# The last expert feed-forward placed among the events of the last attention, gated on its second-layer activations, and row maxima prepared two units ahead

## The reference, cut to what matters

```python
rh = relu(features @ router_w1 + router_b1)
expert_logits = softmax(rh @ router_w2 + router_b2)
top_w, top_i = top_k(expert_logits, 2)
routing_weights = softmax(top_w)
h1 = relu(einsum('bsd,edh->bseh', features, expert_w1) + expert_b1)
h2 = relu(einsum('bseh,ehf->bsef', h1, expert_w2) + expert_b2)
expert_out = einsum('bsef,efo->bseo', h2, expert_w3) + expert_b3
...
combined = sum(sel * routing_weights[..., None], axis=2)
```

## Time and profile before

| what | value |
|---|---|
| three runs | 1465.64, 1471.26, 1472.61 us, median 1471.26 us |
| profiled execution | 1465.17 us, of which the trace spans 1463.1 us |
| busy over the span | PE 80%, DVE 60%, ACT 42%, POOL 42% |
| mean granted clock of TensorE | 0.864 of full speed |
| first attention | from 79 to 860 us |
| second attention | from 940 to 1319 us |
| last feed-forward | from 1319 us to the end |

### The profile page before, as it was taken

How to read it: one execution, slowest core, us unless ns; L and a number is a source line. 1 busy time by engine, 2 the same in 40 slices (tenths; PEclk the granted TensorE clock), 3 DMA queues, 4 the chain that set the end, 5 groups by cost and what they waited for, 6 DMA issues and landing times.

```text
span 1463.1 us, 26112 instructions
## 1 busy us (share of the span) xinstructions
PE 1167.1 (80%) x9805; PEld 769.0 (53%) x9805; DVE 875.2 (60%) x1807; ACT 614.5 (42%) x1249; POOL 608.9 (42%) x1193
## 2 busy tenths in 40 slices
PE   5579999999999999999999937305476674837995
PEld 3345565666666666666666623103264554734663
DVE  3434655655565565655656323146889888732998
ACT  1224555555554545545455413103352524213552
POOL 3201444734545445454554631478534635440000
PEclk9768999999999999999999967657667586666998
DMA  3100000000000000000000011211000000000000
GB/s 79 24 1 1 2 3 2 5 5 2 4 2 2 2 2 3 2 2 2 2 2 2 2 29 61 66 16 17 1 1 0 1 0 1 12 0 0 12 16 16
DMA packets 31369, 14.78 MB, mean 10 GB/s; under 512 B 27522, under 2 KB 28642, under 8 KB 31245
## 3 DMA queue, kind: packets, MB, share of 16 engines
q1 hardware_dynamic: 26637, 11.21, 3.3%
q0 software_dynamic: 4608, 1.91, 1.4%
HBM read 6.72 MB, written 7.27 MB: 10 GB/s over the span
## 4 chain that ended last, share of the span: by engine, by line
PE 63%; DVE 24%; POOL 6%; issue 4%; DMA 2%; ACT 1%; SPq 0%; POOLq 0%; DVEq 0%; ACTq 0%
PE psum L700 20%; PE psum L681 10%; PE psum L609 8%; PE psum L672 7%; PE psum L656 3%; DVE arena L1965 3%; PE psum L594 2%; DVE arena L1964 2%; DVE arena L1959 2%; PE psum L519 1%; POOL lnst L1089 1%; PE psum L614 1%; PE psum L751 1%; PE psum L764 1%; DVE lnst L1613 1%
## 5 line engine op out<-in xcount | busy, mean ns | idle before, releaser
L1355 ACT ACTIVATE arena<-psum 125x500 f32<-125x500 f32 x576 | 306.8, 585 | 342.9 <-PE psum L681 342.9
L1643 DVE TENSOR_REDUCE arena<-psum 125x1 f32<-125x500 f32 x384 | 242.6, 673 | 208.7 <-PE psum L609 208.5
L609 PE MATMUL psum<-arena 32*125 32x500 f32 (+1 forms) x1536 | 324.9, 520 | 0.6 <-ACT arena L1346 0.6
L700 PE MATMUL psum<-arena,XN 125*64 125x250 f32 x2304 | 308.6, 388 | 0.2 <-ACT arena L1355 0.2
L681 PE MATMUL psum<-arena 32*125 32x250 f32 x2304 | 293.9, 371 | 0.0
L681 PEld LDWEIGHTS psum<-arena 32*125 32x125 f32 x2304 | 216.0, 183 | 12.1 <-issue 1.4
L700 PEld LDWEIGHTS psum<-arena,XN 125*64 125x64 f32 x2304 | 140.6, 137 | 123.3 <-issue 78.0
L1646 DVE TENSOR_REDUCE arena<-psum 125x2 f32<-125x500 f32 x192 | 121.4, 674 | 72.6 <-PE psum L609 72.6
L609 PEld LDWEIGHTS psum<-arena 32*125 32x125 f32 x1536 | 128.6, 184 | 3.5 <-issue 2.1
L672 PE MATMUL psum<-arena,onesb 3*125 3x500 bf16 x576 | 123.3, 422 | 5.3 <-DMA arena<-arena 5.3
L1118 POOL TENSOR_SCALAR arena<-arena 125x4 bf16<-125x4 f32 x96 | 21.9, 229 | 217.3 <-DVE arena L1651 215.5
(11 more groups left out here) (327 smaller groups left out, 2079.0 us busy)
## 6 DMA issues: line engine op xcount, KB each, us to landing
arena<-arena SPq DMA_DIRECT2D x192, 1.5 KB
expert_in<-XN SPq DMA_DIRECT2D x8, 256.0 KB, 4.8
arena<-expert_in SPq DMA_DIRECT2D x4, 512.0 KB, 5.1
expert_out<-arena SPq DMA_DIRECT2D x4, 512.0 KB, 2.7
out<-H SPq DMA_DIRECT2D x8, 187.5 KB
expert_in<-XN,slot_in POOLq DMA_INDIRECT x48, 2.5
XN<-expert_out,slot_out POOLq DMA_INDIRECT x48, 3.9
arena<-in_L_ffn_w SPq DMA_DIRECT2D x2, 256.0 KB, 4.2
```

Source lines behind the costliest of these rows:

```text
L609: last = pe.matmul(ps[0:R, at_:at_ + hi - lo], QH[row:row + 32, b, g, j * R:(j + 1) * R], KH[row:row + 32, b, g, lo:hi], start=True, stop= ...
L700: last = pe.matmul(ctx_bank[64 * h2:64 * h2 + 64, 0:THIRD], XN[:, p, c, a, :], PR[:, x % 4, h2, i * THIRD:(i + 1) * THIRD], start=(c == 0) ...
L1355: act.activation(PR[:, x % 4, h2, :], st_bank[(2 * x + h2) % 3][0:R, 0:2 * THIRD], ACT.Exp)\
L1643: dve.reduce_max(MX[:, q % 2, 0, 2 * h2 + tile:2 * h2 + tile + 1], ps[0:R, 0:2 * THIRD], AX)\
```

## The change

The last feed-forward is rewritten and becomes part of `events`. Its work is cut into `router`, `logit` and `gates` for each pair, and 24 steps (pair, half `th`, expert pair `ep`), each for both sequences of the pair. Step `k` has `layer1(k)`, `layer2(k - 1)`, and each third step `layer3`. `layer1` now is two matmuls that use 64 rows of the array each. `layer2` has, ahead of its two matmuls, two that use 32 rows each and spread the gates, transposed before by `gates`, over 128 partitions; DVE multiplies the second-layer activations by them (`gated`). `layer3` sums over experts in PSUM: for each sequence and tile one matmul of 32 rows (gates times `b3r`, the third bias) and three of 128 rows, all of 64 columns. DVE adds the result to `H` once for each half and sequence (`added`). The choice of experts is made for each pair by `choices` and `route`.

`ffn_events` places them: `router`, `logit` and `gates` of pair `p` in the three `x` from `6p + 20` on; steps 0 to 5 at `x` = 23 to 25, steps 6 to 11 at 29 to 31, steps 12 to 17 at 35 to 37, two in each `x`; everything of pair 3 behind them. `room` moves to `x = 16` and does more. In the first attention the maxima of unit 1 stand ahead of step 0, and those of units 2 and 3 earlier.

```diff
-GB, CVB, KSB, GTB, AOB, LNG, LNB, OB, RB2, EB3, WD = (
-    0, 8, 264, 392, 394, 658, 722, 786, 850, 856, 1240)
+GB, CVB, KSB, GTB, AOB, LNG, LNB, OB, RB2, WD = (
+    0, 8, 264, 392, 394, 658, 722, 786, 850, 856)
...
+        ROOM, EARLY, PER = 16, True, 2
+        steps1 = [(p, th, ep) for p in range(NP) for th in range(2) for ep in range(3)]
+        head1 = [(kind, p) for p in range(NP) for kind in ("router", "logit", "gates")]
+        body1 = [("step", k) for k in range(len(steps1) + 2)]
...
+            while head1 and heads < (1 if x is not None else 2):
+                kind, p = head1[0]
+                if x is not None and x <= NJ * (p + 1) + 13:
+                    break
+                events.append(head1.pop(0))
...
-            if x == 3 * NJ:
+            if x == ROOM:
                 events.append(("room", 0))
+            if EARLY:
+                ffn_events(x)
+        ffn_events(None)
...
-            return (k - 3) // 2 if k < 15 else k - 9
+            return (k - 6) // 2 if k < 12 else k - 9
...
-        shift_at = {min(max_step(3 * q + 2) + 2, 3 * q - 1): q for q in range(1, NQ)}
+        shift_at = {min(max_step(3 * q + 2) + 2, 3 * q - 1) if q > 1 else 0: q for q in range(1, NQ)}
...
-        before += [("score", 0, i) for i in range(6)] + [("shift", 0)]
+        before += [("score", 0, i) for i in range(6)] + [("score", 1, i) for i in range(4)] + [("shift", 0)]
+        before += [("score", 1, i) for i in range(4, 6)]
...
+            def layer1(k):
...
+                for a in range(2):
+                    r = slice(64 * a, 64 * a + 64)
+                    ps, done = take(pe, ("l1", k, a))
+                    pe.matmul(ps[:, 0:HALF], e1w[r, ep, :], XT[r, cols], start=True, stop=True,
+                              tile_position=(64 * a, 0)).then_inc(done, 1)
...
+            def layer2(k):
...
+                for a in range(2):
+                    r = slice(64 * a + 32 * (k % 2), 64 * a + 32 * (k % 2) + 32)
+                    ps, done = take(pe, ("gate", k, a))
+                    pe.matmul(ps[:, 0:HALF], SEL[r, ep].rearrange("r e d -> r (e d)"),
+                              GT[r, p % 2, th * HALF:(th + 1) * HALF], start=True, stop=True,
+                              tile_position=(64 * a + 32 * (k % 2), 0)).then_inc(done, 1)
+                for a in range(2):
+                    emptied(pe, ("l1", k, a))
+                    ps, done = take(pe, ("l2", k, a))
+                    pe.matmul(ps[:, 0:HALF], e2w[:, ep, :], H1[(2 * k + a) % 4], start=True, stop=True)\
+                        .then_inc(done, 1)
...
+            def layer3(n):
...
+                    for m in range(3):
+                        o = ps[0:R, m * D:(m + 1) * D]
+                        pe.matmul(o, GT[r, p % 2, (3 * th + m) * R:(3 * th + m + 1) * R], b3r[r, :],
+                                  start=True, stop=False, tile_position=(64 * a, 0))
+                        for ep in range(3):
+                            last = pe.matmul(o, H2[6 * (n % 2) + 2 * ep + a][:, m * R:(m + 1) * R], e3w[:, ep, :],
+                                             start=False, stop=(ep == 2))
...
+                elif kind == "step":
+                    if x < len(steps1):
+                        layer1(x)
+                    if 1 <= x <= len(steps1):
+                        layer2(x - 1)
+                    if x >= 4 and x % 3 == 1:
+                        layer3(x // 3 - 1)
...
-                    pool.memset(e1w, 0.0)
-                    pool.memset(e2w, 0.0)
-                    pool.memset(e3w, 0.0).then_inc(S["late_zero"], 1)
+                    pool.memset(b3r, 0.0)
+                    pool.memset(e2w, 0.0).then_inc(S["late_zero"], 1)
+                    link(pool.memset(GP, 0.0))
...
+                    pool.tensor_scalar(SEL.rearrange("r p e d -> r (p e) d"), over(ramp, 6, D), 0.0, None,
+                                       ALU.is_equal).then_inc(S["select"], 1)
...
+            def gated(k):
...
+                for a in range(2):
+                    emptied(dve, ("l2", k, a))
+                    g, done = filled(dve, ("gate", k, a))
...
+                    dve.tensor_tensor(H2[6 * (n % 2) + 2 * ep + a], H2R[(2 * k + a) % 4], g[:, 0:HALF], ALU.mult)\
+                       .then_inc(done, 1)
```

More of the change, by code:

```diff
@@ L885, in product, with router @@
                     last.then_inc(done, 1)
+            def router(p):
+                if p == 0:
+                    pe.wait_ge(S["w_late"], 16 * 11)
+                for th in range(2):
+                    emptied(pe, ("xt", 3, p, th))
+                for th in range(2):
+                    cols = slice(p * L + th * HALF, p * L + (th + 1) * HALF)
+                    ps, done = take(pe, ("rh", p, th))
+                    pe.matmul(ps[0:64, 0:HALF], W["rw1"], XT[:, cols], start=True, stop=True).then_inc(done, 1)
@@ new lines, in logit, with gates @@
+            def logit(p):
+                for th in range(2):
+                    emptied(pe, ("rh", p, th))
+                ps, done = take(pe, ("lg", p))
+                for j in range(NJ):
+                    last = pe.matmul(ps[0:R, 12 * j:12 * j + 12], RH[0:64, p % 2, j * R:(j + 1) * R], W["rw2"][0:64, :],
+                                     start=True, stop=True)
+                last.then_inc(done, 1)
+            def gates(p):
+                if p == 0:
+                    pe.wait_ge(S["select"], 1)
+                pe.wait_ge(S["route1_pad"], p + 1)
+                for th in range(2):
+                    ps, done = take(pe, ("gt", p, th))
+                    for n in range(3):
+                        j = 3 * th + n
+                        last = pe.transpose(ps[:, n * R:(n + 1) * R],
+                                            GP[:, p % 2, 2 * j:2 * j + 2].rearrange("r a q c -> r (a q c)"),
+                                            ident[0:R, 0:R])
+                    last.then_inc(done, 1)
@@ L918, in _ @@
[L918 to L948, removed]
@@ L950, in _ @@
-            NX = len(units)
-            for x in range(NX + 1):
-                if x < NX:
-                    layer1(x)
-                if x:
-                    layer2(x - 1)
-                    if x >= 6 and x % 3 == 0:
-                        layer3(*units[x - 6][0:3])
-            layer3(*units[NX - 3][0:3])
+                elif kind == "router":
+                    router(x)
+                elif kind == "logit":
+                    logit(x)
+                elif kind == "gates":
+                    gates(x)
+                elif kind == "step":
[5 more added lines that the diff above has]
+                        layer3(x // 3 - 1)
@@ L1880, in _, with added @@
+            def added(n):
+                p, th = divmod(n, 2)
+                for a in range(2):
+                    ps, done = filled(dve, ("l3", n, a))
+                    v = H[:, p, 3 * th:3 * th + 3, a, :]
+                    dve.tensor_tensor(v, v, ps[0:R, 0:3 * D].rearrange("r (j d) -> r j d", d=D), ALU.add)\
+                       .then_inc(done, 1)
             for event in events:
@@ L1972 @@
+                elif kind == "logit":
+                    choices(x)
+                elif kind == "gates":
+                    route(x)
+                elif kind == "step":
+                    if 1 <= x <= len(steps1):
+                        gated(x - 1)
+                    if x >= 4 and x % 3 == 1:
+                        added(x // 3 - 1)
 _INS = ['x', 'L0_tok_conv_w', 'L0_tok_conv_b', 'L0_tok_bn_gamma', 'L0_tok_bn_beta', 'L0_tok_bn_mean',
```

288 lines of the change are left out of this document (176 added, 112 removed).

## The result

The changed kernel takes 1534.93 us (median of 4 runs, 1532.05 to 1541.18), the kernel before 1471.13 beside it: ratio 1.0447, interval 1.0402 to 1.0491. Slower was the likelier direction of the forecast, but the time lies far above its 1480 us and above the upper end of its range, 1502. The profiled execution has a span of 1531.1 us, 59 more than the 1472 of the sum.

What follows compares the result with a forecast made beforehand. The prediction took VectorE to bound the last feed-forward. Its stretches summed to an end at 1482 us, less 10 for the first attention: 1472, 9 above the span of 1463.1; on the median, 1480 us, range for all 1446 to 1502.

Steps and rivals of the forecast that it cites:

- start at half clock 2: In each stretch of steps, TensorE loses 2 us starting at half clock, then runs at full clock.
- Rival 2: TensorE stays at half clock in the inserted stretches, costing 25 us: 1505 us; sign, clock from 1289 under 0.75; chance 0.14.
- Step: One feed-forward step on TensorE, three changes of shape included, takes 3.06 us; a `layer3` takes 6.3 us.
- Waits for the choice of experts: No steps run in `x` = 26 to 28, 32 to 34 and tail routing: 18, 15.5 and 12 us.
- rival 1: Overlap comes cheaper: changes of shape, bubbles' clock and routing chain save 30 us, 1450 us; sign, bubbles under 10; chance 0.31.
- The choice itself: `choices` and `route` on 72 elements, 0.27 us per operation, take 6.9 us, four times.
- The first attention: Earlier maxima remove the transfer wait of step 3 and most of the half clock: gain 10 us, ends 0 and 17.
- `x` = 20 to 22: VectorE-bound attention stretch, lengthened by 6.9 us of choice and 1.3 of gates; `x` = 23 then begins at 1289.
- `room`: Moved ahead of the chunk for which VectorE waits on GpSimd, it adds 3.8 us; ends 1.5 and 6.
- VectorE's relief: In the last feed-forward, VectorE's some 100 us fall to 48 products and 16 additions, 33 us.
- the last of the rivals: Rival 3: no change that can be told, 1471 us, VectorE's relief eaten by 28 us of added TensorE work; chance 0.18.
- some 60 us of nearly idle TensorE: Router, expert choice and last layer norms, 1288 to 1349 us, leave TensorE nearly idle, to be filled by steps.

Runs made afterwards that it cites:

- bias128: The changed kernel with the bias matmul in `layer3` on all 128 rows, zero weights in the others: 1481.66 us, ratio 1.0087 to the kernel before.
- after_held: The changed kernel with its own `layer3` and the steps ordered as in turned_held: 1526.77 us, ratio 1.0358 to the kernel before.
- not_early: The changed kernel with its whole feed-forward behind the attention: 1540.75 us, ratio 1.0502 to the kernel before.
- turned: The changed kernel with `layer3` turned round: weights stationary, 375 columns of `H2` moving, three transposes back: 1467.48 us, ratio 0.9975 to the kernel before.
- cols128: The changed kernel with 128 moving columns in `layer3`, the upper 64 unread padding, row alternation kept: 1504.80 us, ratio 1.025 to the kernel before.
- ahead_only: The kernel before with only the change's earlier maxima in the first attention: 1463.95 us, ratio 0.9955 to the kernel before.
- turned_held: turned with one step per place, gates behind their place's step, steps 15 to 17 spread in the tail: 1454.76 us, ratio 0.9879 to the kernel before.
- no_bias: The changed kernel without the gated third bias in `layer3`, so the output lacks that term: 1471.98 us, ratio 1.0006 to the kernel before.

## Why the prediction was wrong

**The step that failed** is the one that gave every stretch of steps "start at half clock 2" and full clock behind it. Length times clock, for the four stretches: 42.3 x 0.74 = 31.3, 47.8 x 0.71 = 33.9, 46.9 x 0.68 = 31.9, and 58.8 x 0.70 = 41.2 us (1469.2 to 1528.0, clock from a window of its own, below), 138 us of work at full clock; the sum had 136 and 8 for the starts. They took 196 us. So of the 59 us by which the span passed the sum, some 50 are clock.

```profile
1469.20:1528.00 58.80, 57.70 (x225) 0.70 0.04 9
```

The half clock cost 196 - 138, some 58 us, in these stretches. The part at the starts can be read by itself, since each stretch begins at 0.50 and keeps it for 14.7, 6.1 (from 1346.3), 6.9 and 6.1 us:

```profile
1283.10:1297.80 14.70, 14.70 (x57) 9.53 (x56) 3.01 (x8) 4.83 (x11) 0.00 (x0) 0.50 0.00 0
1410.30:1417.20 6.90, 6.90 (x17) 2.69 (x16) 0.78 (x2) 2.68 (x6) 0.00 (x0) 0.50 0.00 0
1469.20:1475.30 6.10, 6.10 (x15) 2.37 (x16) 0.55 (x1) 2.21 (x5) 0.00 (x0) 0.50 0.00 0
```

Half of these 33.8 us, 17, is lost there, where the sum had 8. The other 41 us stand behind falls inside the dense work, for which the sum had nothing. The runs agree: bias128 takes back 53 us, of which 8 x 1.65 = 13 are shorter groups and 40 are clock.

I had argued the clock from density: "from 1277 to 1288, busy all the time, the clock was 0.86". No row of before that I read has narrow matmuls and changes of shape together for several microseconds, so the trace of before neither showed this nor excluded it, and no term of the sum or of the range stood for it. The Trainium skill argues as I did: "TensorE: Matmul & The Clock Gate", section "HAM oscillation — how this bites in real kernels", puts a clock that goes to and fro, in the kernel that it looks at, down to stretches in which the engine waits. The half clock at the starts agrees with that, as each stands behind a wait. The falls inside the dense work do not: from 1410.3 to 1457.2 TensorE was busy 46.9 of 46.9 us, and the clock fell twice and was 0.68 on average.

**Rival 2** gave the right sign and its condition came true: the granted clock from 1289 to 1531 was 0.70, below its 0.75. But its mechanism was another. It laid the half clock to the inserted waits, 25 us. Of that the starts bear out 9 us more than the sum had; the larger part is not theirs, since after_held and not_early, with these waits shortened, keep the falls inside the dense work, and bias128, turned and cols128, with the waits in place, lose them.

```profile
1289.00:1531.00 242.00, 205.24 (x824) 0.70 0.03 7
```

**The other terms of the sum:**

- Step: 3.06 forecast, 3.13 measured; `layer3` 6.3, measured 6.9 at full clock, as a change of shape cost some 0.14 us and not 0.10. Together under 7 us, and the Trainium skill's rule that a change of mode drains TensorE ("TensorEngine Tiling (Array Packing)", section "Key Properties") agrees with the 0.14.
- Waits for the choice of experts: 18, 15.5 and 12 forecast, 21.0, 16.2 and 12.0 measured. Right but for the first, 3 us short. The idle time directly ahead of L964 was 9.60, 7.69 and 6.41 us, though, and not the 10 to 15 that I had named as a sign; being under 10 was to speak for rival 1. It did not: the rest of each wait stands ahead of the logits (L951, idle for 5.80, 2.45 and 0.71 us) and in router and logits themselves, and the waits as a whole were no shorter.
- The choice itself: 6.9 us forecast for each pair. From L2012 to the end of L2050 it took 11.0 us in `x` = 20 to 22 (with 1.4 of attention work in between), 9.5, 7.6 and 6.3 in the tail. In the first three, one to three operations that else take 0.17 to 0.23 us took 1.0 to 1.5. In the second and third choice each of them overlaps a GpSimd operation on `XN` and ends within 0.1 us behind it, as L2019 does below; in the tail, with GpSimd idle, there is none. No run tests whether one causes the other.
- The first attention: 10 forecast, 6.9 measured in the trace and 6.6 by ahead_only, which shows it as a gain of its own.
- `x` = 20 to 22: 6.9 + 1.3 = 8.2 us longer forecast, 10.9 measured (1254.1 to 1283.1, where it was 1258.6 to 1276.7), as the choice was longer. The 12 of the sum has the 3.8 for `room` in it.
- `room`: 3.8 us forecast, 3.9 measured: VectorE's wait for the chunk that opens pair 3, 5.33 us in the earlier trace rows, is now 9.20 us. With the start, `x` = 23 begins 4 us later than the sum had it.
- VectorE's relief was real. Its products and additions, 64 x 0.55 = 35 us by the forecast's own figures (it says 33), took 26.2 and 5.7 us. L2065 is its largest group behind 1283 us, and the engine idled 104.7 us ahead of it. The relief was worth nothing, since TensorE's pace set the end, as the last of the rivals said.

VectorE's wait for the chunk behind `room`, and the long operation of the third choice with the GpSimd operation beside it:

```profile
1232.00 1.04 DVE L1966 TENSOR_REDUCE arena<-arena 125x128 f32<-125x512 f32 x1 [9.20 <-POOL arena L1321]
...
1401.95 1.52 POOL L1175 TENSOR_TENSOR XN<-XN,lnst 125x768 f32<-125x768 f32 x1
...
1402.05 1.50 DVE L2019 TENSOR_TENSOR arena<-arena 125x72 f32<-125x72 f32 x1
```

A reading of mine was wrong as well: "some 60 us of nearly idle TensorE". From 1319 to 1349 TensorE was busy 22.79 of 30 us at 0.62, so that stretch had 7 us of idle time and the one before it 25, some 32 in all. The sum does not use the 60, but rival 1 leaned on it.

**Rival 1**, cheaper overlap, is refuted in its premises (the changes of shape do cost, each stretch starts at half clock, and the choices were no shorter), but the overlap itself is real: 11 and 13 us, once `layer3` leaves the clock alone. With the full clock the forecast's design comes out at 1481.66 us, near the 1480 of the sum; that is in part luck, since its `layer3` is 8 x 1.05 us shorter than the one forecast (its starts at half clock, in turn, are longer than the sum had them).

What stays open: what in the alternating narrow `layer3` the chip's clock answers to. The runs show that either edit suffices, not which quantity they have in common; a run with 32-row matmuls of 64 columns that do not alternate was not made.

## What to carry to other kernels

Busy is not enough to count on the full clock: before adding a block of small matmuls to a dense stretch, find rows of the same shapes in the same alternation, and price the block and what follows it at both levels. Where the moving side is narrow (64 columns here), turn the matmul round so that the wide operand moves; here it took `layer3` from 6.9 to 3.1 us and left the clock up, transposes back included. An idle stretch is filled in part by laying less work in each place and more places, so that something stands between every request and its answer: from turned to turned_held the waits ahead of the last three gates went from 9.6, 7.0 and 6.4 us to 4.1 each, and the time fell by 13 us.

## What the runs showed that I had not expected

A bias matmul of 32 rows by 64 columns, six in each `layer3`, cost the kernel 63 us in 1535 (no_bias). From start to start the eight `layer3` took 70 us with it and 32 without, 38 us less, of which 8 x 2.9 = 23 are there at full clock already. Most of the rest stands in the 375-column matmuls between them, which no edit touched: the mean of L992 went from 669 to 535 ns, in the changed kernel (first) and in no_bias, and L976, L986 and L992 together lost 25 us of busy time. Doubling the columns of `layer3`, which only adds work, made the kernel 30 us faster.

```profile
L992 PE MATMUL psum<-arena 128*128 128x375 f32 x96 | 51.1, 669 | 0.0
```

```profile
L992 PE MATMUL psum<-arena 128*128 128x375 f32 x96 | 39.4, 535 | 0.0
```
